# Self-attention of two batches: keys projected first, VectorE and TensorE orders of the setup rearranged

## The reference

```python
x = x + tanh(g_xattn[0]) * cross_attention_masked(layernorm(x), ctx)   # A, 16 heads, 77 keys
x = x + tanh(g_ffn[0])   * top2_moe(layernorm(x))                      # B, 8 experts
x = x + tanh(g_xattn[1]) * cross_attention(layernorm(x), ctx)          # C, 16 heads, 77 keys
x = x + tanh(g_ffn[1])   * nested_self_attention(layernorm(x))         # D, 8 heads
# D, for token blocks e = 0..3 of 128 tokens each, m = 128 >> e:
#   xn = layernorm(xe, norm_w, norm_b)[..., :m];  q, k, v = xn @ W[:, :m].T + b
#   attn = softmax(q @ k.T * 128**-0.5) over all 512 tokens;  out = attn @ v
#   out_e = out[:, :m] @ o_w[:m, :m].T + o_b[:m], zeros behind it, plus xe
```

## Time and profile before

| what | us |
|---|---|
| median of 3 runs | 259.5 |
| lowest and highest run | 258.45, 260.24 |
| the profiled execution's own time | 258.49 |
| its span, first to last instruction | 256.6 |
| TensorE busy | 225.3 |
| VectorE busy | 115.8 |
| ScalarE busy | 99.2 |
| GpSimd busy | 82.7 |

### The profile page before, as it was taken

How to read it: one execution, slowest core, us unless ns; L and a number is a source line. 1 busy time by engine, 2 the same in 40 slices (tenths; PEclk the granted TensorE clock), 3 DMA queues, 4 the chain that set the end, 5 groups by cost and what they waited for, 6 DMA issues and landing times.

```text
span 256.6 us, 4203 instructions
## 1 busy us (share of the span) xinstructions
PE 225.3 (88%) x1635; PEld 126.9 (49%) x1649; DVE 115.8 (45%) x335; ACT 99.2 (39%) x160; POOL 82.7 (32%) x104
## 2 busy tenths in 40 slices
PE   7878999999979979997999977689898988968984
PEld 2334433344546858875774432324333454546742
DVE  0867236205668401110120984643628855773121
ACT  0522643576155065454420043463750034302631
POOL 2560700004320777777771125100560065000000
PEclk9999999999999999999999999999999999997998
DMA  6999200000230121211113200000000000000011
GB/s 212 403 411 386 63 0 3 0 3 1 82 87 7 40 50 44 45 45 45 50 34 110 74 0 0 3 0 3 0 0 0 4 0 3 0 3 0 3 41 41
DMA packets 10908, 14.72 MB, mean 57 GB/s; under 512 B 1383, under 2 KB 7914, under 8 KB 10890
## 3 DMA queue, kind: packets, MB, share of 16 engines
q1 hardware_dynamic: 9200, 11.29, 12.4%
q0 software_dynamic: 1312, 2.40, 3.8%
q10 hardware_dynamic: 378, 0.78, 1.0%
HBM read 10.82 MB, written 3.93 MB: 57 GB/s over the span
## 4 chain that ended last, share of the span: by engine, by line
PE 64%; DVE 17%; issue 6%; ACT 5%; DMA 4%; POOL 3%; SPq 0%; DVEq 0%; ACTq 0%; POOLq 0%
PE wk L588 8%; PE wk L950 7%; PE ts L900 6%; PE ts L776 5%; PE wk L802 5%; DVE nmx L1345 4%; DVE nmx L1365 3%; PE ts L779 3%; PE ts L766 3%; PE wk L617 2%; DMA pr<-xs_d,src_i 2%; PE wk L698 2%; DMA pk<-in_pk 2%; PE wk L730 2%; PE wk L842 2%
## 5 line engine op out<-in xcount | busy, mean ns | idle before, releaser
L588 PE MATMUL wk<-warm 128*128 128x512 bf16 x152 | 39.5, 397 | 5.0 <-DVE warm L1499 1.4
L473 POOL TENSOR_TENSOR rstd<-ve,half 128x4 f32<-128x4 f32 (+1 forms) x8 | 9.7, 1209 | 87.7 <-DVE ve L1317 87.7
L1181 ACT ACTIVATE pr<-ts 77x1024 f32<-77x1024 f32 x28 | 27.0, 1016 | 20.1 <-PE ts L779 10.3
L588 PEld LDWEIGHTS wk<-warm 128*128 128x128 bf16 x165 | 15.9, 102 | 25.4 <-issue 6.1
L522 POOL DMA_INDIRECT pr<-xs_d,src_i x20 | 20.2, 1011 | 14.0 <-DVE unused L1608 8.2
L1248 ACT ACTIVATE pr<-ts,pk 128x320 f32<-128x320 f32 x32 | 16.6, 528 | 16.7 <-PE ts L900 16.5
L527 POOL DMA_INDIRECT y_d<-onT,dst_i x20 | 20.0, 1001 | 6.1 <-issue 5.5
L950 PE MATMUL wk<-w,pr 128*128 128x128 f32 (+1 forms) x192 | 20.0, 278 | 0.0
L900 PE MATMUL ts<-pr,w 128*128 128x320 f32 x64 | 18.7, 435 | 1.3 <-ACT pr L1241 0.7
L950 PEld LDWEIGHTS wk<-w,pr 128*128 128x128 f32 (+1 forms) x192 | 18.4, 173 | 1.5 <-issue 1.2
L1640 DVE TENSOR_TENSOR onT<-wk,b 128x128 f32<-128x128 f32 x16 | 4.7, 292 | 25.9 <-PE wk L950 25.9
(11 more groups left out here) (240 smaller groups left out, 392.9 us busy)
## 6 DMA issues: line engine op xcount, KB each, us to landing
w<-in_w SPq DMA_DIRECT2D x8, 512.0 KB, 11.7
y_d<-fill SPq DMA_DIRECT2D x1, 1024.0 KB, 11.5
xs_d<-xn SPq DMA_DIRECT2D x4, 256.0 KB, 2.6
pk<-in_pk SPq DMA_DIRECT2D x1, 928.0 KB, 8.5
bpk<-in_bpk SPq DMA_DIRECT2D x1, 517.0 KB, 7.1
x<-in_x SPq DMA_DIRECT2D x2, 256.0 KB, 5.6
sw<-in_sw SPq DMA_DIRECT2D x2, 256.0 KB, 7.9
b<-in_b SPq DMA_DIRECT2D x1, 512.0 KB, 15.0
```

Source lines behind the costliest of these rows:

```text
L473: pool.tensor_tensor(rstd[:, b, 0:n, :], ve[:, b, 0:n, :], half[:, 0:n * TB].rearrange("p (n t) -> p n t", n=n), ALU.pow).then_inc(rstd_re ...
L588: m = pe.matmul(w, warm[:, 0:P], warm[:, :], start=True, stop=True)
L1181: m = act.activation(prs[u][0:NK, r, 2 * i:2 * i + 2, :], src[0:NK], ACT.Exp)
```

## The change

In unit (D, 0), k is projected ahead of q, ScalarE copies k, and VectorE copies q. The maxima groups A and B come directly behind the projections, ahead of the second half of (C, 1)'s values; group D comes ahead of `project_out("C", 1)`, C and E behind it. On VectorE both divisions of (C, 1) come behind the reductions of A and B, and the statistics of (D, 1) come behind the residual of (C, 1), ahead of the reductions of C and E. For (D, 1), the transposes come directly behind `scores_h4(0)`, k is projected ahead of q and before the score round 1, ScalarE copies q between the exponentials of rounds 0 and 1, and VectorE k. Group B of (D, 1) goes from `ts` to four `wk` banks. The value projection of (D, 1) comes behind group D, and its products with the exponentials of (D, 0) are no longer split by group D. Waiting products are put elsewhere. The job list follows.

```diff
@@ job list
-    add("pe", ("fill", "C", 2), ("fill", "C", 3))
+    add("pe", ("fill", "C", 2))
     add("dve", ("xT", "D", 0))
-    add("act", ("pv", "C", 1, 0), ("q", "D", 0), ("k", "D", 0), ("pv", "C", 1, 1))
-    add("dve", ("tm", "C", 1, 0))
+    add("act", ("pv", "C", 1, 0), ("k", "D", 0))
+    add("dve", ("q", "D", 0))
     mxd(0, "A")
-    add("dve", ("tm", "C", 1, 1))
+    add("act", ("pv", "C", 1, 1))
+    add("dve", ("tm", "C", 1, 0), ("tm", "C", 1, 1))
     add("act", ("onT", "C", 1))
+    add("dve", ("y", "C", 1))
     mxd(0, "C")
-    add("dve", ("y", "C", 1))
     mxd(0, "E")
-    add("dve", ("v", "D", 0))
-    add("pe", ("fill", "D", 0))
-    add("dve", ("nT", "D", 0))
+    add("dve", ("v", "D", 0), ("nT", "D", 0))
+    add("pe", ("fill", "C", 3), ("fill", "D", 0))
     add("act", ("h4", 0))
-    add("pe", ("fill", "D", 1), ("fill", "D", 2))
-    add("dve", ("xT", "D", 1), ("q", "D", 1), ("k", "D", 1))
-    add("pe", ("fill", "D", 3))
+    add("dve", ("xT", "D", 1))
+    add("pe", ("fill", "D", 1))
+    add("dve", ("k", "D", 1))
+    add("act", ("q", "D", 1))
+    add("pe", ("fill", "D", 2), ("fill", "D", 3))
     mxd(1, "A")
     mxd(1, "E")
     mxd(1, "C")
+    mxd(1, "B")
     add("dve", ("v", "D", 1))
@@ TensorE
-            fill("C", 3, 1)
             transposes_x("D", 0)
             values("C", 1, 0)
+            project("k", "D", 0)
             project("q", "D", 0)
-            project("k", "D", 0)
+            maxima_d(0, "A", 1)
+            maxima_d(0, "B", 0)
             values("C", 1, 1)
             token_major("C", 1, 0)
-            maxima_d(0, "A", 1)
             token_major("C", 1, 1)
-            maxima_d(0, "B")
             channel_major("C", 1)
-            maxima_d(0, "C")
+            maxima_d(0, "D", 1)
             project_out("C", 1)
-            maxima_d(0, "D")
-            maxima_d(0, "E")
-            project("v", "D", 0)
-            fill("D", 0, 4)
-            transposes_max("D", 0, 3)
+            maxima_d(0, "C", 1)
+            maxima_d(0, "E", 2)
+            project("v", "D", 0, 1)
+            transposes_max("D", 0, 4)
+            fill("C", 3, 2)
+            fill("D", 0, 1)
             scores_h4(0)
+            transposes_x("D", 1)
             scores("D", 0, 0)
-            fill("D", 1, 3)
-            fill("D", 2, 3)
+            fill("D", 1, 1)
+            project("k", "D", 1)
+            project("q", "D", 1)
             scores("D", 0, 1)
-            transposes_x("D", 1)
-            project("q", "D", 1, 2)
-            project("k", "D", 1)
-            scores("D", 0, 2)
-            fill("D", 3, 2)
+            fill("D", 2, 1)
+            fill("D", 3, 1)
             maxima_d(1, "A", 0)
             maxima_d(1, "E", 0)
+            scores("D", 0, 2)
+            maxima_d(1, "C", 2)
             scores("D", 0, 3)
-            maxima_d(1, "C", 0)
+            maxima_d(1, "B", 1)
+            maxima_d(1, "D", 0)
             project("v", "D", 1)
-            maxima_d(1, "B", 0)
             w = bank("pv", "D", 0)
-            values_d(w, 0, 0)
-            values_d(w, 0, 1)
-            maxima_d(1, "D", 0)
-            values_d(w, 0, 2)
-            values_d(w, 0, 3).then_inc(job_mm, 1)
+            for kt in range(TB):
+                m = values_d(w, 0, kt)
+            m.then_inc(job_mm, 1)
             transposes_max("D", 1, 1)
@@ ScalarE
-            act.activation(qT[0][:, :], job("q", "D", 0), ACT.Identity, bias=col("bqD")).then_inc(job_act, 1)
             w = job("k", "D", 0)
...
             exp_h4(0)
-            for r in range(TB):
-                exps("D", 0, r)
+            exps("D", 0, 0)
+            act.activation(qT[1][:, :], job("q", "D", 1), ACT.Identity, bias=col("bqD")).then_inc(job_act, 1)
+            exps("D", 0, 1)
+            exps("D", 0, 2)
+            exps("D", 0, 3)
@@ VectorE
             take_xT2(0)
+            take_q2()
+            take_maxima_d(0, "A")
+            take_maxima_d(0, "B")
             divide("C", 1, 0)
-            take_maxima_d(0, "A")
             divide("C", 1, 1)
-            take_maxima_d(0, "B")
+            take_maxima_d(0, "D")
+            residual("C", 1)
+            norm_stats("D", 1)
             take_maxima_d(0, "C")
-            residual("C", 1)
-            take_maxima_d(0, "D")
             take_maxima_d(0, "E")
             split_maxima("D", 0)
             take_v2(0)
             take_nT("D", 0)
-            norm_stats("D", 1)
             norm("D", 1)
             take_xT2(1)
-            take_q2_k2()
+            take_k2()
```

More of the change, by code:

```diff
@@ L225, with d_heads @@
 assert all(JOB["s", L, b, 0] % 2 == 0 for L, b in WK_ROUNDS) and JOB["mx", "C", 1, 0] % 2 == 0
-assert all(JOB["mxd", b, g, 0] % WKB + len(D_MAX[g]) <= WKB for b in range(B) for g in "AC")
+IN_SCORE_BANKS = [(0, "B"), (0, "D"), (1, "D")]
+def d_heads(b, g):
+    if (b, g) == (1, "B"):
+        at = JOB["mxd", b, g, 0]
+        return [(0, (at + i) % WKB) for i in range(WKB)]
+    return D_MAX[g]
+assert all(JOB["mxd", b, g, 0] % WKB + len(D_MAX[g]) <= WKB for b in range(B) for g in "ACE")
 def taken(n):
@@ L713, in maxima_d @@
             def maxima_d(b, g, wait_products=2):
-                n = len(D_MAX[g])
-                if g in "ACE":
-                    banks = [bank("mxd", b, g, i) for i in range(n)]
[L718 to L723, removed]
+                heads = d_heads(b, g)
+                n = len(heads)
+                if (b, g) in IN_SCORE_BANKS:
+                    banks = [ts[:, i, :] for i in range(n)]
+                    if (b, g) == (0, "D"):
+                        pe.wait_ge(mxd_out, 1)
+                    else:
+                        pe.wait_ge(s_exp, 2 * (s_index("CD"[b], 1 - b, 3) + 1))
+                else:
+                    banks = [bank("mxd", b, g, i) for i in range(n)]
                 keep_warm(banks[0], wait_products)
@@ L727, in maxima_d @@
                     after("k", "D", b)
-                for w, (e, h) in zip(banks, D_MAX[g]):
+                for w, (e, h) in zip(banks, heads):
                     j, v = h % 4, h // 4
                     m = pe.matmul(w, qT[b][32 * j:32 * j + 32, P * e:P * e + P], kd[32 * j:32 * j + 32, b, v, :], start=True, stop=True)
-                if g in "ACE":
+                if (b, g) in IN_SCORE_BANKS:
+                    m.then_inc(mxd_mm, 1)
+                else:
                     m.then_inc(job_mm, n)
-                else:
-                    m.then_inc(mxd_mm, 1)
             def transposes_max(L, b, wait_products=0):
@@ L1331, in take_maxima_d @@
             def take_maxima_d(b, g):
-                heads = D_MAX[g]
-                n = len(heads)
-                if g in "ACE":
+                e, h = D_MAX[g][0]
+                n = len(D_MAX[g])
+                if (b, g) in IN_SCORE_BANKS:
+                    v.wait_ge(mxd_mm, IN_SCORE_BANKS.index((b, g)) + 1)
+                    banks = ts[:, :, :]
+                else:
                     at = JOB["mxd", b, g, 0]
                     v.wait_ge(job_mm, at + n)
-                    banks = wk[:, at % WKB:at % WKB + n, :]
-                else:
-                    v.wait_ge(mxd_mm, 2 * b + (1 if g == "B" else 2))
-                    banks = ts[:, :, :]
-                e, h = heads[0]
+                    banks = wk[:, :, :] if n == WKB else wk[:, at % WKB:at % WKB + n, :]
                 c = H2 * e + 2 * (h % 4) + h // 4
@@ L1345, in take_maxima_d @@
                 m = v.tensor_reduce(dst, banks, AX.X, ALU.max, negate=True)
-                if g in "ACE":
+                if (b, g) in IN_SCORE_BANKS:
+                    m.then_inc(mxd_out, 1)
+                else:
                     m.then_inc(job_dve, n)
-                else:
-                    m.then_inc(mxd_out, 1)
             def take_maxima_c():
@@ L1374, in split_maxima @@
                 if L == "D":
-                    v.wait_ge(*done("mxd", b, "C" if b else "E", 2 if b else 0))
-                    v.wait_ge(mxd_out, 2 * b + 2)
+                    v.wait_ge(*done("mxd", b, "B" if b else "E", 3 if b else 0))
+                    v.wait_ge(mxd_out, 2 + b)
                 elif b == 0:
@@ L1469, in take_xT2, with take_q2, take_k2 @@
                 m.then_inc(job_dve, 1)
-            def take_q2_k2():
-                v.tensor_scalar(qT[1][:, :], job("q", "D", 1), col("bqD"), None, ALU.add).then_inc(job_dve, 1)
+            def take_q2():
+                v.tensor_scalar(qT[0][:, :], job("q", "D", 0), col("bqD"), None, ALU.add).then_inc(job_dve, 1)
+            def take_k2():
                 w = job("k", "D", 1)
```

## The result

The changed kernel takes 260.72 us (median of 8 runs, 260.26 to 261.86) against 258.98 for the kernel before on the same chips (8 runs): the ratio is 1.0086, with a 95% interval of 1.006 to 1.0112. One of the eight runs of the kernel before took 266.46 us, in a slower state, and only the median holds it, not the ratio: without it that median is 258.45. The profiled execution took 260.26 us, its span is 258.3. The forecast was 259.9 within 257.7 to 262.3, no change that could be told; the time is 0.86% longer, on the side of the forecast's small loss, but nearer to the loss of rival 1 (2.0 us) than to the 0.4 us of the forecast.

A forecast was written before the change was run, and what follows sets the result against it. No single engine was the bound; in 197 to 205 us VectorE's reductions were. Stage 0's +2.5 and stage 1's -2.2 gave +0.3 us, the clock +0.1: 259.5 + 0.4 = 259.9 us, range 257.7 to 262.3.

The forecast's parts named there:

- rival 1: An extra fall of the clock at 205.5 to 209 us, behind the holes around E: 261.5 us, chance 0.25.
- Stage 0, DVE's path: VectorE from 185 us to (D, 0)'s h4 products: A reduced from 191.35, 2.1 us idle ahead of D, E ends 205.95.
- v behind C's reduction: Before (D, 0)'s h4: v's product shares a bank with group C's first pair, so waits for C's reduction, until 205.5.
- Stage 0's term: 185 us to the start of (D, 0)'s h4 products, 206.12 before: 2.5 us longer, h4 at about 208.6.
- Stage 1's term: From (D, 0)'s h4 products to (D, 1)'s, 26.38 us before: 24.15 us, 2.2 shorter.
- The clock term: New holes before (D, 0)'s h4 against a possibly avoided fall in the tail: balanced at a small loss, +0.1 us.
- rival 2: Tail behind (D, 1)'s h4: its fall of the clock goes away, -1.1 us, 258.8 us; chance 0.2.

## Why the prediction was right, and where it was off

- *Stage 0, DVE's path*: right. A's reduction 191.35 forecast, 191.21 measured; the idle time ahead of D 2.1 and 2.13; E's end 205.95 and 205.55. The cause that was named (`channel_major` behind the second division, D behind `channel_major`) stands in the trace as the wait of 1.52 us.
- *v behind C's reduction*: right as a wait (1.60 us), but its price, 0.7 us of the sum, was overstated. With v out of the way h4 came only 0.24 us earlier.
- *Stage 0's term, +2.5 us*: with the clock held it was 208.14 - 206.12 = 2.0, 0.5 less; as it ran, 3.5.
- *Stage 1's term, -2.2 us*: measured -1.8 (24.56 for 26.38; 24.61 with stage 0 filled), 0.4 less. The steps are there one by one: B waits for C's reduction, v for B's by 1.62 us (1.0 in the forecast), the four value products follow at 0.9 us each, and VectorE waits 2.26 us for the transposes of the maxima. With both stages exchanged alone, each half of the trade was shown. That the sum still gave 232.8 where 232.75 was measured with the clock held is luck: the two terms were off by 0.5 and 0.4 us, and the errors cancel.
- *The clock term, +0.1 us*: this is the step that failed. I let a new fall in stage 0 and the end of the fall in the tail balance. The fall in stage 0 came, at the place of rival 1 and behind the holes that it named, and cost 1.5 us (1.6 forecast). The fall in the tail did not go (rival 2) in the profiled execution, though the idle time ahead of h4 was shorter, 1.21 us. Whether it comes is not settled by the program: of seven traces with an unfilled tail, five have it, and two, of kernels with the same stage 1 as the changed one, do not (the run with the holes around E filled, and the one with the old stage 0). None of the seven traces with a filled tail has it. The Trainium skill ("TensorE: Matmul & The Clock Gate", section "HAM oscillation — how this bites in real kernels") has the rule that gaps between bursts cost the clock again in the next burst, and the trace agrees, at 205.9, though the gaps here are shorter than those of the page's example; no run here tells the transposes, which the prediction named with it, from the idle time beside them. I had given this rival 0.25. The trace of before spoke both ways. Its only place with two such waits close together, 1.50 us ahead of 230.89 and 1.21 us ahead of 232.50, had lost the clock, and stage 0 was to get three new holes of 0.8 to 1.9 us. But single waits of 1.54, 1.31 and 1.24 us (ahead of 117.29, 151.76 and 156.82) had kept it.
- *The forecast*, 0.4 us slower, has the right side and is too small. In the traces, the 0.2 us left of the two stages (2.0 and 1.8) and the fall's 1.5 make the 1.7 us by which (D, 1)'s h4 starts later. Between the medians it is 1.74 us with all runs, and 2.3 without the far run of the kernel before; the 0.5 us more aren't traced. The range held because it was 4.6 us wide and took in most of rival 1, not because the clock's term was right.
- Not settled: how often each of the holes takes the clock down. One profiled execution stands for each kernel, and the falls differ between them. Some lie in parts that no edit touches: at 74 us in three traces of the fourteen, at 152 in one.

## What to carry to other kernels

When work is moved ahead of a wait, count the holes that it leaves on TensorE as well as the time on the path: here a trade of +2.0 against -1.8 us was level, and a fall of the clock behind a new hole of 1.6 us made it a loss of 1.7. Waiting products in an idle bank, put where the engine waits anyway, repaid more (0.6% on the kernel before) than any reordering here was shown to, and narrowed the spread there; but no more of them than the wait holds (two fewer gave 0.4 us). When an edit moves work and a fall of the clock goes at the same time, compare with a run that only holds the clock: moving the statistics looked like a gain of 1.7 us and was none. And when several copies count in one semaphore, look at who waits for the later one.

## What the runs showed of the hardware

- The granted clock fell behind idle stretches that are short. In the run with the old stage 0 and the new stage 1, it fell at 207.6, when TensorE had been idle for 0.4 us only; ahead of that lay the h4 products and a wait of 0.62 us ahead of them. Most of the long wait for xn came behind the fall, and the clock stayed down until 214.4. Whether a hole takes the clock down also depends on the execution. The same 1.31 us of waiting ahead of 151.6, in a stretch that no edit touches, had a fall at 152.0 behind it in the run with the old stage 1 and none in the kernel before or the changed one; and two kernels that are the same up to 230 us had a fall at 196.5 and none.
- VectorE's normalising took longer beside GpSimd's additions of two tensors. GpSimd's timeline of the changed kernel (VectorE's row, at 209.09, stands above):

```profile
208.77 1.26 POOL L579 TENSOR_TENSOR xb<-xb,x 128x512 f32<-128x512 f32 x1
```

The four instructions from 209.09 took 2.09 us there, and 1.17 before, where each took 0.34 to 0.39. Here the first took 1.02 us and ended 0.08 us behind GpSimd's addition (208.77 to 210.03). The second took 0.61 and ended 0.08 us behind the next addition (L582, 210.11 to 210.57). The run with the old stage 1 has both again: 0.76 and 0.61 us, each ending 0.08 us behind an addition. Beside GpSimd's tensor_scalar instructions, in the kernel with the holes around E filled, the four took 1.17. The Trainium skill ("SBUF — State Buffer", section "Who interferes with whom") describes the port pair that the two engines share as an exclusive lock for a whole instruction; the trace agrees for these additions, and shows no such wait beside the tensor_scalar instructions. It cost nothing here, as TensorE came to the transposes at 210.92.
